# Splitting the FFN weights during the first token block instead of ahead of attention, in a transformer layer on eight cores

## What is computed

```python
kv = x @ Wkv_down.T                       # rank 64
scores = q @ (kv @ Wk_up.T) / 16; out = softmax(scores) @ (kv @ Wv_up.T)
x = layernorm(x + out @ Wo.T)
# m1, m2: outer products of 16 rows of x
h = x @ W1.T + scale * x @ m1.T + b1      # W1: 4096 x 1024
h = gelu(h)
x = layernorm(x + h @ W2.T + scale * h @ m2.T + b2)   # W2: 1024 x 4096
```

## Time and profile before

| | us |
|---|---|
| two runs | 4517.38 and 4838.07 |
| their median | 4677.72 |
| the profiled execution | 4568.37 |
| its span, slowest core (core 1) | 4566.8 |
| spans of the other cores | 4488.1 to 4553.2 |
| PE busy in the span | 3062.0 (67%) |
| POOL busy | 525.4 (12%) |
| ACT busy | 507.6 (11%) |
| DVE busy | 739.9 (16%) |

### The profile page before, as it was taken

One profiled execution on the slowest core, in us unless ns is written; L12 is line 12 of the kernel. 1 busy time (PEld: TensorE's weight loads), 2 busy tenths in 40 slices (PEclk: granted clock), 3 DMA queues, 4 the chain that ended last, 5 costly groups with the idle time before them and its releaser, 6 DMA issues.

```text
span 4566.8 us, 33138 instructions; the slowest of 8 cores (4488.1 to 4566.8 us)
## 1 busy us (share of the span) xinstructions
PE 3062.0 (67%) x10610; PEld 1194.4 (26%) x10610; DVE 739.9 (16%) x1123; ACT 507.6 (11%) x729; POOL 525.4 (12%) x1124
## 2 busy tenths in 40 slices
PE   4600001475000988989989828998899889978997
PEld 1400000121000332323323203442344234423342
DVE  1100000111001112112121132201320142013201
ACT  0000000000000432423324201100100010001000
POOL 2333332233332000000000000000000000000000
PEclk8555555666555999999999959998899889988798
DMA  5533333222222001001010022233223232323232
GB/s 150 136 76 71 75 85 74 54 53 58 59 58 64 5 5 38 6 3 41 6 38 5 4 74 74 70 96 89 84 70 97 83 88 71 96 60 87 57 93 65
DMA packets 548348, 287.51 MB, mean 63 GB/s; under 512 B 133250, under 2 KB 526466, under 8 KB 547154
## 3 DMA queue, kind: packets, MB, share of 16 engines
...
## 4 chain that ended last, share of the span: by engine, by line
PE 58%; DMA 11%; POOL 9%; ACTq 9%; DVE 5%; issue 4%; ACT 2%; DVEq 0%; POOLq 0%
PE psU L654 10%; ACTq L270 5%; POOL wspb L255 5%; POOL wspb L262 4%; DMA wspb<-wspf 4%; ACTq L249 4%; DMA wspf<-w2p 3%; PE psY L686 3%; PE psY L946 3%; PE psY L951 3%; PE psY L956 3%; PE ps L620 3%; PE psY L1045 2%; PE ps L1045 2%; DMA wspf<-w1p 2%
## 5 line engine op out<-in xcount | busy, mean ns | idle before, releaser
L654 PE MATMUL psU<-et,kvtok 128*65 128x512 f32 x1024 | 523.1, 598 | 2.6 <-ACT et L640 0.4
L361 PE MATMUL ps<-wst,wkus 128*64 128x512 f32 x64 | 50.6, 938 | 561.5 <-DVE qtf L369 545.5
L640 ACT ACTIVATE et<-ps,Ubias 128x512 f32<-128x512 f32 x512 | 352.9, 689 | 643.1 <-PE psU L654 431.3
L255 POOL DMA_DIRECT2D wspb<-wspf x512 | 272.3, 539 | 812.8 <-DMA wspf<-w2p 430.6
L976 ACT ACTIVATE hgf<-htmp,b1s 128x512 f32<-128x512 f32 x128 | 92.7, 724 | 1316.5 <-DVE htmp L970 1316.5
L441 PE MATMUL psY<-U,ones1r 1*128 1x1 f32 x16 | 4.4, 342 | 343.8 <-DVE U L438 340.9
L946 PE MATMUL psY<-z1s,whl 128*128 128x512 bf16 x512 | 212.6, 415 | 15.1 <-DVE u_bc L939 15.1
L262 POOL TENSOR_TENSOR wspb<-wspf,wspb 128x128 bf16<-128x128 f32 x512 | 203.2, 423 | 155.9 <-DMA wspb<-wspf 155.9
L951 PE MATMUL psY<-z1s,whl 128*128 128x512 bf16 x512 | 212.4, 415 | 0.0
L956 PE MATMUL psY<-z1s,whl 128*128 128x512 bf16 x512 | 210.9, 412 | 0.0
L946 PE MATMUL ps<-z1s,whl 128*128 128x512 bf16 x512 | 201.0, 393 | 0.0
...
## 6 DMA issues: line engine op xcount, KB each, us to landing
whl<-w1sd SPq DMA_DIRECT2D x1024, 64.0 KB, 2.0
whl<-w2sd SPq DMA_DIRECT2D x1024, 64.0 KB, 2.0
wspf<-w1p ACTq DMA_DIRECT2D x256, 64.0 KB, 2.2
wspb<-wspf POOLq DMA_DIRECT2D x512, 32.0 KB, 1.8
w1sd<-wspb ACTq DMA_DIRECT2D x256, 64.0 KB, 1.7
wspf<-w2p ACTq DMA_DIRECT2D x256, 64.0 KB, 2.1
w2sd<-wspb ACTq DMA_DIRECT2D x256, 64.0 KB, 1.7
...
```

The source lines that it names most:

```text
L255: P.op("gpsimd", lambda e, c=c, sl=sl: e.dma_start(out=wspb[:, sl * 2048 + c * 256: sl * 2048 + c * 256 + 128], in_=wspf[:, sl * 1024 + c ...
L640: P.op("scalar", lambda e, kc=kc, par=par, h=h: e.activation(out=et[:, par * 512:(par + 1) * 512], in_=psA[par][:], func=AF.Exp, bias=Ubia ...
L654: P.op("tensor", lambda e, kc=kc, par=par, h=h: e.matmul(psU[h % 2][:], kvtok[:, kc * 65:(kc + 1) * 65], et[:, par * 512:(par + 1) * 512], ...
```

## The change

The split is taken out of stage 1 and done in stage 3 while tb = 0 runs. For tb = 0, `plan_w1` loads the float32 block into one of three new buffers (eight DMAs on SP's queue), converts it with one DMA of 128 x 1024 on POOL's queue straight into the slot of whl1 from which the matmuls read, and subtracts with one POOL instruction of 1024 columns. The matmuls wait for that subtraction. After the block's matmuls are planned, `plan_w1_store` writes hi and lo parts to HBM in separate DMAs of 128 rows of 128 columns, 16 for a W1 block, on the scalar engine's queue, ahead of the block's gelu. A slot is overwritten only after its matmuls and its stores are done. W2 goes the same way with half the sizes (four loads, a cast and a subtraction of 512 columns, eight stores). The lookahead at tb = 0 is three blocks instead of four. For tb > 0 loads from HBM are as before, except that they wait for the stores of their own slot. The DMAs into BT and U8 move from the scalar engine's queue to POOL's. The layouts in HBM stay; in the slots of tb = 0 the hi parts lie together and the lo parts behind them.

```diff
-    wspf = es_kv.enter_context(nc.sbuf_tensor("wspf", [128, 2 * 1024], F32, side="right"))
-    wspb = es_kv.enter_context(nc.sbuf_tensor("wspb", [128, 2 * 2048], BF16, side="right"))
     qtl_t = es_kv.enter_context(nc.sbuf_tensor("qtl_t", [128, 4 * T], BF16, side="right"))
...
-        sSST = [sems["sST0"], sems["sST1"]]
-        split_blocks = ([("w1", hc) for hc in range(HCN)]
-                        + [("w2", gi) for gi in range(64)])
-        spl = {"i": 0, "sub": {}, "st": {}}
-
-        def plan_split_block():
-            if spl["i"] >= len(split_blocks):
-                return
-            kind, idx = split_blocks[spl["i"]]
-            sl = spl["i"] % 2
-            spl["i"] += 1
-            if kind == "w1":
-                nch = DC
-                src_ap = lambda c, idx=idx: w1p[idx, c * 128:(c + 1) * 128, :]
-                dst_ap = lambda c, idx=idx: w1sd[idx, c * 128:(c + 1) * 128, :]
-            else:
-                d, g = divmod(idx, 8)
-                nch = 4
-                src_ap = lambda c, d=d, g=g: w2p[d, (g * 4 + c) * 128:(g * 4 + c + 1) * 128, :]
-                dst_ap = lambda c, d=d, g=g: w2sd[d, (g * 4 + c) * 128:(g * 4 + c + 1) * 128, :]
-            for c in range(nch):
-                P.op("scalar", lambda e, c=c, sl=sl, src_ap=src_ap: e.dma_start(
-                    out=wspf[:, sl * 1024 + c * 128: sl * 1024 + (c + 1) * 128],
-                    in_=src_ap(c)),
-                    waits=[(cG, spl["sub"].get(sl, 0))], inc=sSLD[sl], inc_k=16)
-            vL = sSLD[sl].n
-            for c in range(nch):
-                P.op("gpsimd", lambda e, c=c, sl=sl: e.dma_start(
-                    out=wspb[:, sl * 2048 + c * 256: sl * 2048 + c * 256 + 128],
-                    in_=wspf[:, sl * 1024 + c * 128: sl * 1024 + (c + 1) * 128]),
-                    waits=[(sSLD[sl], vL), (sSST[sl], spl["st"].get(sl, 0))],
-                    inc=sSCA[sl], inc_k=16)
-            vC = sSCA[sl].n
-            for c in range(nch):
-                P.op("gpsimd", lambda e, c=c, sl=sl: e.tensor_sub(
-                    wspb[:, sl * 2048 + c * 256 + 128: sl * 2048 + (c + 1) * 256],
-                    wspf[:, sl * 1024 + c * 128: sl * 1024 + (c + 1) * 128],
-                    wspb[:, sl * 2048 + c * 256: sl * 2048 + c * 256 + 128]),
-                    waits=[(sSCA[sl], vC)], inc=cG)
-            spl["sub"][sl] = cG.n
-            cGv = cG.n
-            for c in range(nch):
-                P.op("scalar", lambda e, c=c, sl=sl, dst_ap=dst_ap: e.dma_start(
-                    out=dst_ap(c),
-                    in_=wspb[:, sl * 2048 + c * 256: sl * 2048 + (c + 1) * 256]),
-                    waits=[(cG, cGv)], inc=sSST[sl], inc_k=16)
-            spl["st"][sl] = sSST[sl].n
 
         for tb in range(NQB):
...
-                plan_split_block()
         cV_A = cV.n
...
+                P.op("gpsimd", lambda e, h=h, d2=d2: e.dma_start(
                     out=BT[(h % 2) * 64:(h % 2) * 64 + 64,
                            (h // 2) * D + d2 * 512:(h // 2) * D + (d2 + 1) * 512],
-                    in_=bstage[0:64, :]), waits=[(cV, cV_bst)], inc=sBT2, inc_k=16)
-                dS_bst = sBT2.n
+                    in_=bstage[0:64, :]), waits=[(cV, cV_bst)], inc=sBT, inc_k=16)
+                dS_bst = sBT.n
             wst_free[h % 2] = cT.n
             if h + 2 < H:
                 plan_wst(H + h + 2, woT)
-            for _ in range(3):
...
-        while spl["i"] < len(split_blocks):
-            plan_split_block()
-        SPL_T = [(sSST[0], sSST[0].n), (sSST[1], sSST[1].n)]
         cV_qnorm = cV.n
         for p in range(4):
-            P.op("scalar", lambda e, p=p: e.dma_start(
...
 
-        dS_BT_done = sBT2.n
+        dS_BT_done = sBT.n
...
         whl1 = es_ffn.enter_context(nc.sbuf_tensor("whl1", [128, 4 * DC * 256], BF16, side="right"))
+        w2f = es_ffn.enter_context(nc.sbuf_tensor("w2f", [128, 3 * 4 * 128], F32, side="right"))
         whl2 = es_ffn.enter_context(nc.sbuf_tensor("whl2", [128, 4 * 4 * 256], BF16, side="right"))
...
         def plan_w1(tb, hc):
+            s = hc % 3
             s4 = hc % 4
+            if tb > 0:
+                for c in range(DC):
+                    P.op("sync", lambda e, hc=hc, c=c, s4=s4: e.dma_start(
+                        out=whl1[:, s4 * 2048 + c * 256: s4 * 2048 + (c + 1) * 256],
+                        in_=w1sd[hc, c * 128:(c + 1) * 128, :]),
+                        waits=[(cT, w1_free[s4]), (sST[s4], sST_tot[0][s4])],
+                        inc=sW1[s4], inc_k=16)
+                dS_w1[(tb, hc)] = sW1[s4].n
+                return
             for c in range(DC):
-                P.op("sync", lambda e, hc=hc, c=c, s4=s4: e.dma_start(
-                    out=whl1[:, s4 * DC * 256 + c * 256: s4 * DC * 256 + (c + 1) * 256],
-                    in_=w1sd[hc, c * 128:(c + 1) * 128, :]),
-                    waits=[(cT, w1_free[s4])] + SPL_T,
-                    inc=sW1[s4], inc_k=16)
-            dS_w1[(tb, hc)] = sW1[s4].n
+                P.op("sync", lambda e, hc=hc, c=c, s=s: e.dma_start(
+                    out=w1f[:, s * DC * 128 + c * 128: s * DC * 128 + (c + 1) * 128],
+                    in_=w1p[hc, c * 128:(c + 1) * 128, :]),
+                    waits=[(cG, cG_w1.get((tb * HCN + hc) - 3, 0))],
+                    inc=sW1[s], inc_k=16)
+            dS_w1[(tb, hc)] = sW1[s].n
+            P.op("gpsimd", lambda e, s=s, s4=s4: e.dma_start(
+                out=whl1[:, s4 * 2048: s4 * 2048 + 1024],
+                in_=w1f[:, s * DC * 128:(s + 1) * DC * 128]),
+                waits=[(sW1[s], dS_w1[(tb, hc)]), (cT, w1_free[s4]),
+                       (sST[s4], st1_done.get(s4, 0))],
+                inc=sW1C[s % 2], inc_k=16)
+            dS_w1c[(tb, hc)] = sW1C[s % 2].n
+            P.op("gpsimd", lambda e, s=s, s4=s4: e.tensor_sub(
+                whl1[:, s4 * 2048 + 1024: s4 * 2048 + 2048],
+                w1f[:, s * DC * 128:(s + 1) * DC * 128],
+                whl1[:, s4 * 2048: s4 * 2048 + 1024]),
+                waits=[(sW1C[s % 2], dS_w1c[(tb, hc)]), (cT, w1_free[s4])], inc=cG)
+            cG_w1[tb * HCN + hc] = cG.n
+
+        def plan_w1_store(hc):
+            s4 = hc % 4
+            cGv = cG_w1[hc]
+            for c in range(DC):
+                P.op("scalar", lambda e, hc=hc, c=c, s4=s4: e.dma_start(
+                    out=w1sd[hc, c * 128:(c + 1) * 128, 0:128],
+                    in_=whl1[:, s4 * 2048 + c * 128: s4 * 2048 + (c + 1) * 128]),
+                    waits=[(cG, cGv)], inc=sST[s4], inc_k=16)
+                P.op("scalar", lambda e, hc=hc, c=c, s4=s4: e.dma_start(
+                    out=w1sd[hc, c * 128:(c + 1) * 128, 128:256],
+                    in_=whl1[:, s4 * 2048 + 1024 + c * 128:
+                             s4 * 2048 + 1024 + (c + 1) * 128]),
+                    inc=sST[s4], inc_k=16)
+            st1_done[s4] = sST[s4].n
...
         def plan_w2(tb, d, g):
...
+                out=whl2[:, s4 * 1024: s4 * 1024 + 512],
+                in_=w2f[:, s * 512:(s + 1) * 512]),
+                waits=[(sW2[s], dS_w2[(tb, d, g)]), (cT, w2_free[s4]),
+                       (sSU[s4], st2_done.get(s4, 0))],
+                inc=sW2C[s % 2], inc_k=16)
+            dS_w2c[(tb, d, g)] = sW2C[s % 2].n
+            P.op("gpsimd", lambda e, s=s, s4=s4: e.tensor_sub(
...
+        def plan_w2_store(d, g):
+            gi = d * 8 + g
+            s4 = gi % 4
+            cGv = cG_w2[gi]
+            for k in range(4):
+                P.op("scalar", lambda e, d=d, g=g, k=k, s4=s4: e.dma_start(
+                    out=w2sd[d, (g * 4 + k) * 128:(g * 4 + k + 1) * 128, 0:128],
+                    in_=whl2[:, s4 * 1024 + k * 128: s4 * 1024 + (k + 1) * 128]),
+                    waits=[(cG, cGv)], inc=sSU[s4], inc_k=16)
+                P.op("scalar", lambda e, d=d, g=g, k=k, s4=s4: e.dma_start(
+                    out=w2sd[d, (g * 4 + k) * 128:(g * 4 + k + 1) * 128, 128:256],
+                    in_=whl2[:, s4 * 1024 + 512 + k * 128:
+                             s4 * 1024 + 512 + (k + 1) * 128]),
+                    inc=sSU[s4], inc_k=16)
...
 
-            for pf in range(4):
+            if tb == 1 and sST_tot[0] is None:
+                sST_tot[0] = [x.n for x in sST]
...
-                    ww = [(sW1[s4], dS_w1[(tb, hc)]), (cV, cV_z1s), (cV, cV_ubc)]
+                    if tb == 0:
+                        hi1 = s4 * 2048 + c * 128
+                        lo1 = s4 * 2048 + 1024 + c * 128
+                        wwt = (cG, cG_w1[tb * HCN + hc])
+                    else:
+                        hi1 = s4 * 2048 + c * 256
+                        lo1 = s4 * 2048 + c * 256 + 128
+                        wwt = (sW1[s4], dS_w1[(tb, hc)])
+                    ww = [wwt, (cV, cV_z1s), (cV, cV_ubc)]
...
-                    plan_w1(tb, hc + 4)
+                if tb == 0:
+                    plan_w1_store(hc)
+                adv1 = 3 if tb == 0 else 4
```

(3 more changed lines are left out.)

94 lines of the change are left out of this document (58 added, 36 removed).

## The result

| | before | after |
|---|---|---|
| median of all runs, us | 4698.60 (10 runs) | 3872.95 (11 runs) |
| the profiled execution, us | 4568.37 | 3855.79 |
| its span, slowest core, us | 4566.8 (core 1) | 3854.2 (core 3) |
| mean granted clock of that core | 0.810 | 0.893 |

The forecast was 3900 us, with 3800 to 4090 as range.

The account below looks back on a forecast made before the run. The serial weight split over POOL and ACT was taken to bound the first third, delaying DMAs queued behind it. 4568.4 - 893 + 105 - 9.5 + 132 = 3903, say 3900 us; range 3800 to 4090.

Parts of the forecast that it names:

- The front, -893: Stage 1 up to attention: BT loop 556 us shorter, wait before U8's DMAs 335 us shorter, first loads 2 us.
- The step on the BT loop: Stage 1: sixteen groups at 4.58 us, BT's transfer covered by the matmul (about 3.9 without that cover); 556 us less.
- keep their 257 us: Stage 1: the sixteen projection groups take as long as before, PE and DVE waiting only for each other.
- W1, +105: First FFN quarter: ACT's 16 stores and gelu set 8.2 us a block; with extras 296 us, last gelu 105 us later.
- The chain of a cut: W1, blocks 8, 16, 24: u_bc, matmuls and 0.8 us against 7.4 of stores, 6.5 us each, 20 in all.
- T1, -9.5: Between W1 and W2: T1 matmuls mostly fit PE's waiting; 9.5 us remain of 19 because W2's cast queues on POOL.
- W2, +132: First FFN quarter: POOL's turn is longest, taken as 4.8 us a block, 307 us against 175 before.
- The later quarters, 0: FFN after the first quarter: nothing changes, three quarters of 450 us as before.
- The DMA-bound one: Rival, chance 0.20: first-quarter stores at 52 ns a packet make DMA engines the bound; 4088 us in all.
- Hidden better: Rival, chance 0.13: first-quarter POOL turn 3.4 us, W2 bound by ACT's 3.7; 3822 us at most.
- The chain that would have made it slower: Rival, chance 0.02: first-quarter source slots don't overlap; blocks run serially at 32.7 us (W1), 18.5 (W2); 5530 us.
- The low clock: First FFN quarter: PE at 1.2 GHz throughout adds 59 us in W1 and 26 in W2, 3985 us in all.

Follow-up runs that it names:

- e1: Original kernel with only the BT and U8 transfers moved from ScalarE's queue to SyncE's, splits left in stage 1: ratio 0.986 to the original.
- e10: Original kernel with the BT, U8 and two kv transfers all on SyncE's queue, splits left in stage 1: ratio 0.986 to the original.
- e2: Changed kernel with the BT and U8 transfers back on ScalarE's queue: ratio 0.850 to the original, against 0.853 for the changed kernel.
- e3: Changed kernel with one store for hi and lo instead of two, halving store issues, rows still 256 bytes: ratio 0.832 to the original.
- e9: Changed kernel with W1's cast and subtraction on VectorE instead of GpSimd, still 16 stores a block: ratio 0.845 to the original.
- e8: Changed kernel with W2's first three splits ahead of the four transfers waiting for T1 on GpSimd's queue: ratio 0.849 to the original.
- e4: Changed kernel with W2's cast and subtraction on VectorE instead of GpSimd: ratio 0.842 to the original.
- e5: Changed kernel with both splits on VectorE and one store for hi and lo, in two rows of 256 bytes: ratio 0.808 to the original.
- e7: As e5, with hi and lo side by side so a store writes one row of 512 bytes: 3632 and 3637 us.

## Why the prediction was right

The number came within 1.2% of the profiled execution, and the mechanism that it took for the likeliest is the one that the runs show. Its terms are less exact than its sum.

**The front, -893, measured -920** (on the slowest cores; by the medians of the cores -906). The step on the BT loop holds: 77.1 us for 73.6, though not by the group of 4.58 us that it counted on. TensorE's clock came up to 2.4 GHz in the loop (1.90 us for four passes instead of 3.65), so the matmul no longer covered the transfer, the case that the text had in brackets with 3.9 us; the groups took 4.8 on the mean, as a copy sometimes waited for the transfer (39.8 us in nine waits). The step that failed is the one on the projections: "keep their 257 us". They took 232, as they ran at a mean clock of 0.82 instead of 0.69; that is 24 of the 27 us. The text had argued with the clock in the first quarter alone. What decides the clock here is open. In before two cores (2 and 3) had 0.80 in the projections and took 236 to 237 us, behind the same idle stretches as the six others with 0.68 to 0.73 and 251 to 260. All cores of after, e1 and e10, where the BT loop has no such idle stretches, had 0.80 to 0.82, and cores 0 to 3 of e2 0.78 to 0.83.

**That everything of the front goes at once.** The forecast was right, but it named ACT's queue for both waits and did not name POOL's, where e1 found a gate of its own, nor the exponentials behind the stores (e10). It did no harm because the change takes the splits out of both queues; in that the forecast had luck. The waits of the earlier trace rows alone would give e1 the 550 to 850 us of its rival, and about 65 came.

**W1, +105, measured +119.** ACT as the bound is shown by e3 and e9. The failed step is the price of the issues, 8.2 us a block with the gelu: it was 9.3. Of this, 16 issues and the gelu by themselves are 8.7 us on the mean (e9; 8.5 by the median), 0.5 more than put; POOL's work beside them makes the rest, 13 us over W1 by e9, near the 10 kept for "meeting the DMA engines". The chain of a cut was put at 13.8 us and was 13.7, but the text set it against the 7.4 us of stores where it replaces a whole period: 20 in all, measured 14. POOL's own price was put too high and decided nothing: 6.9 us a block, where the first ones took 5.6 to 5.8 (a landing after 3.6 us instead of 4.3, a subtraction of 2.12 instead of 2.4).

**T1, -9.5, measured +3.9.** The mechanism was named, with its price of 9.5 us from T1's end; the failed step is that T1 ends with the last gelu. Two of T1's four groups run in TensorE's pauses, but the other two (48 matmuls, to 2154.3 in after) came behind it:

```profile
2140.58 0.68 DVE L1045 COPY r<-ps 4x512 f32<-4x512 f32 x1 [0.17 <-DVE hplo L1018]
2141.40 0.59 PE L1033 MATMUL ps<-hphi,odd4h 128*4 128x512 bf16 x1 [4.07 <-DVE r L1045]
```

The third group writes where the first had, and waits for VectorE's copy of that; the copy is planned behind the split of the last gelu. POOL's queue stood behind all of it. e8 takes POOL's part out and measures 14.4, where the forecast comes to 9.6.

**W2, +132, measured +116 on the slowest core and +101 by the median of the cores.** POOL's turn was put at 4.8 us and is 4.3 to 4.6: a landing 3.2 us after the issue instead of 2.9, and a subtraction of 1.15 instead of 1.3; little was needed of the 0.4 us kept for the other queues. That POOL is the bound, and ACT the next with 3.7, is what e4 shows (3.9 a block).

**The later quarters, 0, measured -31,** from before's own execution, as shown above. Without it the sum of the forecast would lie 16 us, and not 47, above the span. That it comes so near is partly luck: W1 and T1 came out 28 us above their terms, the projections and W2 41 below.

**The rivals.** The DMA-bound one (0.20) took 26 ns for a 256 B packet and up to 52 by the rule. Trace: 17.5 ns in after (0.257 x 293 x 16 / 68802, q10 in 1827 to 2120 us), so the three queues together came to 0.63 and not to the 0.9 of the sum; and e5 moved the same rows at a share of 0.86 without cost in W2. The Trainium skill (DMA: Bandwidth & Descriptors, Specifications) says that transfers under 512 B are read, modified and written. Two packets of 256 B took 35.4 ns in e5 and one of 512 B took 25.5 in e7, 1.39 times as much for the same bytes, in line with a penalty but not with twice the price. "Hidden better" (0.13) had the mechanism of W2 that e4 had to build first. The chain that would have made it slower didn't form: 6.3 us a block on the mean of all 96, where the text says about 14 for the point at which nothing is gained; its own terms give (893 + 373)/96 = 13.2. It also has 0.02 for this case in one place and 0.015 + 0.015 in another. The low clock, the top of the forecast's own range, didn't decide either: 0.81 was granted in W1 and 0.94 in W2, with PE busy for about two thirds of both.
